# A gated cross-attention block with experts, one core of Trainium2: the output projection as seven products of blocks in place of eight

## Reference, cut to what matters

```python
xn = layernorm(x)                       # x: 8 batches, 100 rows, 1024 columns
q = rms_norm((xn @ Wq) by 32 heads)     # heads of 128
k, v = ([ctx, xn] @ Wk, Wv) by 8 groups # ctx: 8 batches, 361 rows; k is normed
a = softmax(q k^T / sqrt(128)) v        # 4 heads share a group
x = x + tanh(g0) * (a @ Wo)             # a: 800 x 4096, Wo: 4096 x 1024
h = layernorm(x)
x = x + tanh(g1) * experts(h)           # top 2 of 8 low-rank experts
```

## Time and profile before

| what | value |
|---|---|
| runs | 1743.57, 1743.88, 1744.35 us |
| profiled execution | 1743.77 us, its span 1741.9 us |
| PE busy | 1692.7 us, 97% of the span, 9312 matmuls |
| DVE, ACT, POOL busy | 1177.3, 880.9, 716.8 us |
| granted clock of PE | mean 0.991 of full |
| DMA | 278.13 MB, mean 160 GB/s |
| chain that ended last | PE 88%, DVE 4%, DMA 3%, ACT 2% |

### The profile page before, as it was taken

How to read it: one execution, slowest core, us unless ns; L and a number is a source line. 1 busy time by engine, 2 the same in 40 slices (tenths; PEclk the granted TensorE clock), 3 DMA queues, 4 the chain that set the end, 5 groups by cost and what they waited for, 6 DMA issues and landing times.

```text
span 1741.9 us, 26303 instructions
## 1 busy us (share of the span) xinstructions
PE 1692.7 (97%) x9312; PEld 1513.5 (87%) x9312; DVE 1177.3 (68%) x2074; ACT 880.9 (51%) x1655; POOL 716.8 (41%) x584
## 2 busy tenths in 40 slices
...
GB/s 193 156 182 235 236 212 242 158 120 192 153 181 154 143 222 148 104 131 127 120 119 119 131 131 131 122 123 121 131 144 124 219 212 168 218 212 191 195 102 66
DMA packets 215654, 278.13 MB, mean 160 GB/s; under 512 B 51956, under 2 KB 187956, under 8 KB 210020
## 3 DMA queue, kind: packets, MB, share of 16 engines
...
q10 hardware_dynamic: 576, 6.55, 0.9%
...
## 4 chain that ended last, share of the span: by engine, by line
PE 88%; DVE 4%; DMA 3%; ACT 2%; issue 2%; POOL 0%; SPq 0%; DVEq 0%; ACTq 0%; POOLq 0%
PE bank L757 26%; PE bank L759 25%; PE bank L758 25%; PE bank L895 5%; PE bank L862 2%; DMA kT_d<-kst 2%; PE bank L791 1%; PE bank L1045 1%; DMA at_raw<-at_d 1%; DMA kT<-kT_d 1%; ACT w_hi L1111 1%; DMA wr<-Wkv 0%; ACT w_hi L1102 0%; DVE w_lo L1459 0%; PE bank L799 0%
## 5 line engine op out<-in xcount | busy, mean ns | idle before, releaser
L739 POOL TENSOR_SCALAR pr<-pr,rr 100x461 f32<-100x461 f32 x256 | 369.2, 1448 | 300.5 <-DVE rr L1667 300.5
L757 PE MATMUL bank<-w_hi,a_hi 128*128 128x512 f32 (+1 forms) x856 | 341.3, 399 | 12.2 <-DVE a_lo L1442 8.7
L759 PE MATMUL bank<-w_hi,a_lo 128*128 128x512 f32 (+1 forms) x856 | 335.4, 392 | 0.0
L758 PE MATMUL bank<-w_lo,a_hi 128*128 128x512 f32 (+1 forms) x856 | 335.1, 391 | 0.0
L1295 ACT ACTIVATE pr<-bank,nm,rq 100x461 f32<-100x461 f32 x256 | 188.5, 737 | 154.7 <-DVE nm L1658 151.3
L1652 DVE TENSOR_REDUCE mx<-bank 100x1 f32<-100x461 f32 x256 | 161.7, 632 | 82.0 <-PE bank L759 76.8
L757 PEld LDWEIGHTS bank<-w_hi,a_hi 128*128 128x128 f32 (+1 forms) x856 | 158.0, 185 | 49.6 <-issue 9.8
L759 PEld LDWEIGHTS bank<-w_hi,a_lo 128*128 128x128 f32 (+1 forms) x856 | 158.0, 185 | 38.0
L757 PE MATMUL bank<-at_hi,wo_hi 128*128 128x400 f32 x512 | 183.3, 358 | 6.8 <-DVE at_lo L1683 4.1
L757 PE MATMUL bank<-xT_hi,wq_hi 128*128 128x400 f32 x512 | 188.3, 368 | 0.6 <-issue 0.6
L758 PEld LDWEIGHTS bank<-w_lo,a_hi 128*128 128x128 f32 (+1 forms) x856 | 158.3, 185 | 34.8
...
## 6 DMA issues: line engine op xcount, KB each, us to landing
wo_raw<-Wo SPq DMA_DIRECT2D x32, 1024.0 KB, 5.2
...
```

The lines of the kernel that those rows point to most:

```text
L739: pool.tensor_scalar(pr[0:NQ, u % 2, i], pr[0:NQ, u % 2, i], rr[0:NQ, i:i + 1], None, ALU.mult).then_inc(p_done, 1)
L757: pe.matmul(o, lh, rh, start=start, stop=False, skip_group_check=more)
L758: pe.matmul(o, lh, rl, start=False, stop=False, skip_group_check=more)
L759: return pe.matmul(o, ll, rh, start=False, stop=stop, skip_group_check=more)
```

## The change

Tokens (two halves th) and heads (two halves gh of four groups) and columns (two halves) make 2x2 blocks, and the eight block products become seven: P1 = A11 B11, P7 = S3 T3, P5 = S1 T1, P6 = S2 T2, P4 = A22 T4, P2 = A12 B21, P3 = S4 B22, each of 4 chunks of the same 48 matmuls, in this order but P5 and P6 in turn: chunks 0 to 3, 4 to 7, 8 to 15, 16 to 19, 20 to 23, 24 to 27. S1 = A21 + A22, S2 = S1 - A11, S3 = A11 - A21 and S4 = A12 - S2 are made on POOL (chunk_sums) from at_raw and at_more, chunk by chunk; S2 is stored to s2_d and loaded again for P3. T1 to T4 are sums of weight blocks (weight_sum): 64 POOL ops of 128x512 in 16 steps, each with a load of 1 MB into tb and a store of 1 MB to wt_d; 12 ops come before slot 0, one after each of slots 0 to 51. P5 and P4 use banks 4 to 7. The accumulators are combined by DVE adds and three POOL adds of 128x1600 (and one of 128x800). P1 and P7 run in the slots. The second half of the batches is complete first: the experts of batches 4 to 7 (batch_of) stand between the half chunks of P2 and P3 (FFN_AT), those of batches 0 to 3 in the tail, whose order changes. Slot 55 (bare_slot) makes the splits of chunk 0 after its attention work. The expert weights and first x rows are loaded after chunk 16's loads, not at the end of the slots.

```diff
+GQ = G // 2
+CHUNKS = ([(P1, c) for c in range(GQ)] + [(P7, c) for c in range(GQ)] + [(o, c) for c in range(GQ) for o in (P5, P6)] +
+          [(o, c) for o in (P4, P2, P3) for c in range(GQ)])
+FIRST_OF = {o: CHUNKS.index((o, 0)) for o in range(7)}
+LAST_OF = {o: CHUNKS.index((o, GQ - 1)) for o in range(7)}
+
+A_OF = {P1: ((0, 0),), P7: ((0, 0), (1, 0)), P5: ((1, 0), (1, 1)), P6: ((0, 0),), P4: ((1, 1),), P2: ((0, 1),), P3: ((0, 1),)}
+LOADS = {P1: 2, P7: 3, P5: 3, P6: 2, P4: 2, P2: 2, P3: 3}
+SUMMED = (P7, P5, P6, P3)
+
+WT_OF = {P6: 0, P4: 1, P7: 2, P5: 3}
+WT_OPS = ((2, 3, 2, True), (0, 2, 0, False), (3, 3, 0, True), (1, 1, 0, True))
+WT_STEPS = GQ * R
+WT_FIRST = 3
...
+UPPER = (P5, P4)
+TAIL0 = FIRST_OF[P2]
+
+FFN_AT = {}
+for _t in range(B // 2):
+    for _i, _a in enumerate((0, 2, 3, 4, 5)):
+        FFN_AT.setdefault(4 * _t + _a, []).append((_i, _t))
...
+        def out_loaded(m):
+
+            return 16 * sum(LOADS[CHUNKS[n][0]] for n in range(m % 2, m + 1, 2))
+
+        def summed(m):
+
+            return R * sum(o in SUMMED for o, c in CHUNKS[:m + 1])
...
             def load_chunk(m):
-                th, nh, g = chunk_of(m)
+                o, c = CHUNKS[m]
                 k = m % 2
-                if m >= 2:
+                if m < 2:
+                    sp.wait_ge(t_stored[k], 16 * WT_STEPS // 2)
+                else:
                     sp.wait_ge(wo_lo_done, split_after(m - 2))
-                for i in range(2):
-                    sp.wait_ge(ao_stored[i], stored(g * B + th * TB + 2 + i))
-                if m >= 2:
-                    load_chunk_weights(m)
-                sp.dma_start(at_raw[k][:], at_d[g, TB * th:TB * th + TB].rearrange("b p q -> p b q")).then_inc(wo_in[k], 16)
+                if m == FIRST_OF[P7]:
+                    sp.wait_ge(q_done, 2 * H)
+                for th, gh in A_OF[o]:
+                    for i in range(2):
+                        sp.wait_ge(ao_stored[i], stored((GQ * gh + c) * B + th * TB + 2 + i))
+                if o in WT_OF:
+                    w = wt_d[WT_OF[o], c]
+                else:
+                    w = Wo[int(o == P3), c if o == P1 else GQ + c]
+                sp.dma_start(wo_raw[:, k], w).then_inc(wo_in[k], 16)
+
+                if m >= 2 and CHUNKS[m - 1][0] in SUMMED:
+                    sp.wait_ge(at_sum, summed(m - 1))
+                if m == LAST_OF[P6] + 2:
+                    sp.wait_ge(s2_stored, 16 * GQ)
+                dst = [at_raw[k][:], at_more[:, k]]
+                if o == P6:
+                    dst = dst[1:]
+                for (th, gh), to in zip(A_OF[o], dst):
+                    sp.dma_start(to, at_d[GQ * gh + c, TB * th:TB * th + TB].rearrange("b p q -> p b q")).then_inc(wo_in[k], 16)
+                if o == P3:
+                    if c == 0:
+                        sp.wait_ge(s2_stored, 16 * GQ)
+                    sp.dma_start(at_more[:, k], s2_d[c]).then_inc(wo_in[k], 16)
...
+            def store_s2(c):
+                sp.wait_ge(at_sum, summed(FIRST_OF[P6] + 2 * c))
+                sp.dma_start(s2_d[c], at_raw[1][:]).then_inc(s2_stored, 16)
+
+            def load_t(n):
+                if n >= 2:
+                    sp.wait_ge(t_stored[n % 2], 16 * (n // 2))
+                sp.dma_start(tb[:, n % 2], Wo.rearrange("n (k c) p r d -> c r p (n k) d", k=2)[n // R, n % R]).then_inc(t_in[n % 2], 16)
+
+            def store_t(n):
+                sp.wait_ge(t_sum, 4 * n + 4)
+                sp.dma_start(wt_d.rearrange("t c p r d -> c r p t d")[n // R, n % R], tb[:, n % 2]).then_inc(t_stored[n % 2], 16)
...
+            load_t(0)
+            load_t(1)
...
+                if n in (2, 4, 7):
+                    store_t((2, 4, 7).index(n))
+                if n in (3, 5, 8):
+                    load_t(2 + (3, 5, 8).index(n))
...
+                n = u // 4 + WT_FIRST - 1
+                if u >= 4 and u % 4 == 0 and n < WT_STEPS:
+                    store_t(n)
+                if u >= 4 and u % 4 == 1 and n + 2 < WT_STEPS:
+                    load_t(n + 2)
+                if u in (OUT0 - 3, OUT0 - 2):
+                    load_chunk(u - OUT0 + 3)
+            store_s2(0)
+            load_chunk(G + 2)
...
+            for m in range(G + 3, FIRST_OF[P3]):
+                if CHUNKS[m - 1][0] == P6:
+                    store_s2(CHUNKS[m - 1][1])
                 load_chunk(m)
-            for c in range(2 * G):
-                t = c // 4
-                load_chunk(2 * G + c)
-                if c % 4 == 0 and t >= 1:
-                    sp.wait_ge(x1_done, 2 * t)
-                    load_res(t + 1)
-                if c % 4 == 3 and t >= 1:
-                    store(t - 1)
+                if m == FIRST_OF[P4]:
+                    sp.wait_ge(pv_done, UNITS)
+                    sp.dma_start(ar[:], AR).then_inc(ffn_in, 16)
+                    sp.dma_start(bm[:], BmT).then_inc(ffn_in, 16)
+                    load_res(0)
+                    load_res(1)
...
+            next_res(0)
+            load_chunk(FIRST_OF[P3])
+            load_chunk(FIRST_OF[P3] + 1)
+            next_res(1)
+            load_chunk(FIRST_OF[P3] + 2)
+            store(0)
+            load_chunk(FIRST_OF[P3] + 3)
+            next_res(2)
+            store(1)
+            store(2)
...
+            def weight_sum(i):
+
+                n = i // 4
+                to, a, b, minus = WT_OPS[i % 4]
+                if i % 4 == 0:
+                    pool.wait_ge(t_in[n % 2], 16 * (n // 2 + 1))
+                elif i % 4 < 3:
+                    pool.wait_ge(t_sum, i)
+                pool.tensor_tensor(tb[:, n % 2, to], tb[:, n % 2, a], tb[:, n % 2, b],
+                                   ALU.subtract if minus else ALU.add).then_inc(t_sum, 1)
+
+            def chunk_sums(m):
+
+                o, c = CHUNKS[m]
+                k = m % 2
+                pool.wait_ge(wo_in[k], out_loaded(m))
+                if o == P6:
+                    pool.wait_ge(at_sum, summed(m - 1))
+                    pool.wait_ge(wo_lo_done, split_after(m - 2))
+                    if c:
+                        pool.wait_ge(s2_stored, 16 * c)
+                for i in range(R):
+                    q = slice(i * NQ, (i + 1) * NQ)
+                    pool.tensor_tensor(at_raw[k][:, :, q], at_raw[0 if o == P6 else k][:, :, q], at_more[:, k, :, q],
+                                       ALU.add if o == P5 else ALU.subtract).then_inc(at_sum, 1)
+
+            for i in range(4 * WT_FIRST):
...
+                weight_sum(i)
...
+                if u + 4 * WT_FIRST < 4 * WT_STEPS:
+                    weight_sum(u + 4 * WT_FIRST)
+                if FIRST_OF[P7] <= u - OUT0 + 1 <= LAST_OF[P7]:
+                    chunk_sums(u - OUT0 + 1)
+            for m in range(FIRST_OF[P5], LAST_OF[P6] + 1):
+                chunk_sums(m)
+
+            first, second = (slice(0, C // 2), slice(C // 2, C))
+            pool.wait_ge(oT_dve, 10)
+            pool.wait_ge(oT_act, 6)
+            pool.tensor_tensor(oT_late[:, first], oT_late[:, first], oT_early[:, second], ALU.add).then_inc(mix_done, 1)
+            pool.tensor_tensor(oT_early[:, second], oT_early[:, second], oT_late[:, second], ALU.add).then_inc(mix_done, 1)
+            pool.wait_ge(mix_done, 2)
+            pool.tensor_tensor(oT_late[:, second], oT_late[:, second], oT_late[:, first], ALU.add).then_inc(mix_done, 1)
...
+                if t == 2:
+                    chunk_sums(FIRST_OF[P3])
+                    chunk_sums(FIRST_OF[P3] + 1)
+                    pool.wait_ge(oT_act, 8)
+                    pool.tensor_tensor(oT_early[:, 2:4], oT_early[:, 2:4], c_tmp[:], ALU.add).then_inc(mix_done, 1)
+                if t == 3:
+                    chunk_sums(FIRST_OF[P3] + 2)
+                    chunk_sums(FIRST_OF[P3] + 3)
...
+                if i == c == 0 and half != 1:
+                    if o == P1:
+                        pe.wait_ge(ms_done, 2 * G)
+                        pe.wait_ge(pT_lo_done, 4 * OUT0)
+                    if o == P5:
+                        pe.wait_ge(pT_lo_done, 4 * UNITS)
+                        pe.wait_ge(exp_done, 4 * UNITS)
+                    if o in (P7, P6, P4):
+                        done = {P7: 2, P6: 4, P4: 6}[o]
+                        pe.wait_ge(oT_dve, done)
+                        pe.wait_ge(oT_act, done)
+                    if o == P2:
+                        pe.wait_ge(oT_dve, 10)
+                    if o == P3:
+                        pe.wait_ge(oT_dve, 16)
+                        pe.wait_ge(oT_act, 8)
...
+            def bare_slot(u):
+                scores(u, 0)
+                turn_probs(u - 1, 0)
+                scores(u, 1)
+                turn_probs(u - 1, 1)
+                squares(2 * H - 1)
+                scores(u, 2)
+                values(u - 1, 0)
+                turn_probs(u - 1, 2)
+                scores(u, 3)
+                values(u - 1, 1)
+                turn_probs(u - 1, 3)
```

(23 more changed lines are left out.)

299 lines of the change are left out of this document (168 added, 131 removed).

## The result

The changed kernel took 1811.8 us (median of 4 runs, 1806.3 to 1826.5), the kernel before 1743.97: a ratio of 1.040, with an interval of 1.034 to 1.047. It is slower by 68 us where I forecast 9. The profiled execution took 1806.34 us (span 1804.5), 62.6 more than that of before.

A forecast was written before the change was run, and what follows sets the result against it. PE, busy 97% of the span, was taken as the bound. Terms from -35.3 to +30.3 summed to +9.0, less 0.3 for a transpose: +8.7 on the median of 1743.88, so 1752.6 us, range 1735 to 1767.

The forecast's parts named there:

- Four chunks less: Output projection: 32 chunks become 28, each 8.83 us of PE time, so -35.3 us.
- waits gone: Output projection: waits before chunks 8 and 16 and the gap at late chunk 10 lose their place, -7.4 us.
- The chain: Chunks 8 to 15: loads and POOL's sums in series take 28.3 us a pair against PE's 17.7; +30.3 us.
- The mixing on POOL: Chunks 16 to 19: three POOL adds of accumulators run beside them, due only at chunk 20; costs nothing.
- P3 (+3.5): P3's four chunks: load, POOL sums and splits in series, half overlapped; +3.5 us, bounds 0 to 9.
- the tail (-3): Tail: accumulator adds and one batch's gates join, but DVE's idle stretches are filled; -3 us, bounds -5 to +3.
- The start: Start of query phase: head 4's Wq lands about 693.0 behind t stores and load; +16.4 us, bounds 11 to 20.
- Query slots: 52 query slots: one more POOL sum each can hold up DVE's nm; kT has room; +4 us.
- 0.2 as a sign of being wrong: Query slots: the forecast called itself wrong if slots lengthen by more than 0.2 us.
- The rival of 1767: Query phase: POOL's sum holds DVE in every slot, 52 x 0.35 = 18 us instead of 4; chance 0.12.
- Last slots: Last attention slots: P7's chunks load 0.82 MB more and SP's wait delays kT; +2 us, bounds 0 to 7.
- The order of slot 55: Slot 55: the chunk's splits move behind the attention's work; -1.5 us, bounds -4 to +1.

The follow-up runs named there:

- e16_dve56: Changed kernel with start, query slots, chunk loads, mixing and SP's last-slot order rearranged, sums of chunks 8 to 15 on DVE: 1715.8 us, 0.984 of the kernel before.
- e4_chain: Changed kernel with SP's order in chunks 8 to 17 altered: most loads no longer wait for sums, S2 store behind next loads; 1.030 of the kernel before.
- e2_place: Changed kernel with each query slot's weight sum on POOL moved ahead of the slot's four scales; 1.040 of the kernel before.
- e3_t_load: Changed kernel with t loads moved behind kT's load, into slots where no load of Wq stands; 1.029 of the kernel before.
- e5_oneop: Changed kernel with slot weight sums from the thirteenth on replaced by one-operand POOL multiplications of the same size and place; 1.040 of the kernel before.

## Why the prediction was wrong

The sum came to +8.7; the traces differ by 62.6. Of the 53.9 between them, 23.0 lie in the query slots, 14.8 in slots 53 to 62, 10.4 from slot 63 on and 8.4 in the start, less the 2.7 by which the part ahead was shorter.

- **Four chunks less (-35.3)** and the **waits gone (-7.4)**: right as far as can be seen. e16_dve56, without late chunks, takes 38.3 us less than before from slot 63 on.
- **The chain (+30.3)**: right in mechanism and size. 25.2 us of waits before chunks 10 to 16, with groups of 6.1 us, 2.1 of the wait before chunk 17, and 2.0 and 2.6 us of lower clock behind the two large ones. e4_chain and e16_dve56 confirm it from two sides.
- **The mixing on POOL ("nothing")**: wrong, 3.8 us of the wait before chunk 17, with 1.9 us of lower clock behind that wait. I had asked when the adds are due, not what DVE does beside them.
- **P3 (+3.5) and the tail (-3)**: inside their bounds, P3 by luck. Its waits of 1.3, 2.0 and 1.4 us come to 4.7, but none is for P3's heads: two are for y, held through four of POOL's sums, and one for a copy of accumulators. From the last projection matmul on it takes 0.8 us less. With the mixing and the clock the part from slot 63 on came to -1.8 where the terms gave -12.
- **The start (+16.4)**: right in mechanism, short in size: 24.8, above my bound of 20. Wq's landing was forecast to 0.5 us (692.5 against 693), or to 2 us on the clock of before, and so close only because two misses cancel: t2 was asked for at 680.4, not 684, and t2, the second store and Wq took 12 us from there, not 9. But I let PE run until 681.5, and it ran dry at 676.4 (679 on that clock), because I read that from ACT's square and not from PE's last matmul. Head 5, late by the same queue, cost 2.6 more.
- **Query slots (+4, bounds 0 to 11)**: the step that failed most, 27.0 measured, 0.5 a slot, where I had set 0.2 as a sign of being wrong. I named both places, and priced the wrong operation in one and nothing in the other. For POOL's sum I priced DVE's nm, the shortest operation, while the earlier trace rows already showed what a DVE split with two SBUF inputs does next to a sum; the weight split stands at the sum's place in every second slot. 26 x 0.43 = 11 us would have come out; e2_place shows that it is this, and 12.1 us were left of it in e3_t_load. That my bound of 11 for nm is the same number is chance. For kT I wrote that it had room, "if barely where a Wq load stands there too", and stopped: t loads come every fourth slot, Wq loads every second, and as placed they always meet: 14.9 us. The rival of 1767 had the right place and the first of the two causes, at 0.12, though in every slot and not in every second.
- **Last slots (+2, bounds 0 to 7)**: 15.3 together with slot 55, 18.0 without it. 11.5 of it are slot 60 alone. The bounds held the loads, not POOL's sums against the splits that stand beside them, nor the copy that waits behind such a split. The order of slot 55 (-1.5) was about right: slots 54 to 56 took 2.7 us less than before. Some 6 us remain in e16_dve56: a wait of 3.9 us for kT at slot 53 and 2.2 us for the copy, with the clock behind them. No run tried those alone.
- My range ended at 1767, and even all upper bounds together give 1792, because each term was bounded by the rows of its own operation. In two of the stages the change added an operation to POOL next to a DVE operation on the path, and data to a queue ahead of kT.

By the lock of the Trainium skill (SBUF - State Buffer, SBUF: two separate sides), a DVE op with two SBUF inputs waits for a GpSimd op that reads SBUF if that started first, and the other way round. The weight split agrees: in the changed kernel it waits for a sum that started first, and the next POOL operation waits for it (2.03 us); in e5_oneop it starts first and POOL's one-operand operation waits (2.37). Two things don't fit the words "started first". The split of 4.72 us has its start 0.29 us ahead of the first of the four sums that it waits for. And the query split of the kernel before, begun 0.17 us behind a scale of 1.44, took 0.90 and was over before the scale. nm, which by the same rule could wait for a whole sum, took 0.21 us in the mean (0.27 before): it seldom meets one.
